# A ranking split in two: 14 of 16 rounds on the first 240 channels, and another order in an image's last tile

## What is computed

```python
x: (4, 256, 256, 256) float32                        # images, channels, rows, columns
v = _gn(x)                                           # group norm over 32 groups of 8 channels
s = 0.5 * (|dv/dx| + |dv/dy|) + 0.5 * |v|            # differences with [-1, 0, 1], zero padding
sp = s averaged over patches of 32 x 32              # 64 patches, a score for each channel
mask = 1 where a channel is among the 128 best of 256 in its patch, else 0
out = x + v * mask
```

## Time and profile before

| | |
|---|---|
| median of 3 timed runs | 2008.84 us (2007.42 to 2009.37) |
| the profiled execution's own time: its span | 2002.3 us |
| busy: PE, DVE, ACT, POOL | 69%, 77%, 81%, 78% of the span |
| DMA | 780.77 MB, mean 390 GB/s |
| the rankings: first `max` of each image | 382.2, 847.2, 1312.5 and 1773.0 us |

### The profile page before, as it was taken

The page is one execution under the profiler, slowest core; times in us unless marked ns, Lnnn a source line. Parts: engine busy times, 40 slices in busy tenths (PEclk is TensorE's granted clock), DMA queues, the critical chain, the costliest instruction groups (busy, mean ns, idle before and its releaser), DMA issues.

```text
span 2002.3 us, 16132 instructions
## 1 busy us (share of the span) xinstructions
PE 1380.7 (69%) x3528; PEld 675.7 (34%) x3528; DVE 1542.1 (77%) x2087; ACT 1629.1 (81%) x2437; POOL 1555.6 (78%) x1113
## 2 busy tenths in 40 slices
PE   5989989868768867857787687768688876820000
PEld 2444444434333433423333333334333333410000
DVE  7878898789898869879898977888888977872110
ACT  4999999898879888888898879889789887851643
POOL 7899899768787777758877868758878786746776
PEclk9999999988889878879888788889788887965555
DMA  5899899999999999998999999999999999969997
GB/s 252 330 399 369 333 360 392 354 403 424 429 432 430 422 362 433 390 415 365 428 430 429 432 399 389 433 389 386 430 430 432 426 400 390 381 267 397 397 368 270
DMA packets 72082, 780.77 MB, mean 390 GB/s; under 512 B 21883, under 2 KB 21883, under 8 KB 35648
## 3 DMA queue, kind: packets, MB, share of 16 engines
q1 hardware_dynamic: 40896, 723.54, 87.3%
q0 software_dynamic: 31104, 56.45, 7.5%
HBM read 568.33 MB, written 329.25 MB: 448 GB/s over the span
## 4 chain that ended last, share of the span: by engine, by line
issue 20%; DMA 19%; DVE 17%; POOL 16%; ACT 15%; PE 9%; DVEq 3%; POOLq 1%; ACTq 0%; SPq 0%
DVE stats L911 8%; DMA again<-in_x_dram 8%; POOL pair L349 5%; DMA ring<-in_x_dram 4%; ACT again L803 4%; DMA out_dram<-again 4%; DVE sums L938 4%; PE vertical L707 4%; ACT thrown L872 4%; PE vertical L709 4%; POOL pair L355 3%; DVEq L902 3%; ACT vertical L866 3%; DMA ring<-in_x_dram,pair 2%; POOL scratch L349 2%
## 5 line engine op out<-in xcount | busy, mean ns | idle before, releaser
L707 PE MATMUL vertical<-ring,plus 128*128 128x512 f32 (+1 forms) x1200 | 664.4, 638 | 241.9 <-ACT vertical L866 240.9
L349 POOL TENSOR_TENSOR pair<-ring 128x960 f32<-128x960 f32 x360 | 638.3, 1793 | 26.0 <-DVE scratch L1082 17.9
L709 PE MATMUL vertical<-ring,minus 128*128 128x512 f32 (+1 forms) x1200 | 634.0, 612 | 0.0
L911 DVE BATCH_NORM_STATS2 stats<-ring 128x6 f32<-128x512 f32 x960 | 582.4, 680 | 40.4 <-DMA ring<-in_x_dram 31.9
L872 ACT ACTIVATE thrown<-ring,record 128x1024 bf16<-128x1024 f32 x480 | 548.2, 1142 | 8.8
L938 DVE TENSOR_REDUCE sums<-pair 128x2 f32<-128x1920 f32 (+1 forms) x212 | 455.0, 2146 | 126.8 <-POOL pair L349 126.2
L803 ACT ACTIVATE again<-again,coef 128x1024 f32<-128x1024 f32 x324 | 374.4, 1227 | 107.2 <-DMA again<-in_x_dram 106.9
L707 PEld LDWEIGHTS vertical<-ring,plus 128*128 128x128 f32 x1200 | 240.9, 211 | 514.6 <-ACT vertical L866 292.4
L355 POOL TENSOR_TENSOR pair<-ring 128x960 f32<-128x960 f32 x120 | 270.5, 2254 | 141.8 <-DVE sums L938 116.3
L709 PEld LDWEIGHTS vertical<-ring,minus 128*128 128x128 f32 x1200 | 250.0, 208 | 295.5 <-issue 295.5
L349 POOL TENSOR_TENSOR scratch<-ring 128x960 f32<-128x960 f32 x120 | 215.3, 1794 | 152.8 <-ACT kept L822 103.3
(11 more groups left out here) (118 smaller groups left out, 1443.2 us busy)
## 6 DMA issues: line engine op xcount, KB each, us to landing
ring<-in_x_dram SPq DMA_DIRECT2D x59, 4096.0 KB, 20.4
again<-in_x_dram SPq DMA_DIRECT2D x89, 2048.0 KB, 16.6
out_dram<-again SPq DMA_DIRECT2D x89, 2048.0 KB, 16.3
out_dram<-in_x_dram SPq DMA_DIRECT2D x29, 2048.0 KB, 28.6
kept<-in_x_dram SPq DMA_DIRECT2D x4, 4096.0 KB, 22.7
out_dram<-kept SPq DMA_DIRECT2D x8, 2048.0 KB, 13.8
ring<-in_x_dram SPq DMA_DIRECT2D x4, 1024.0 KB, 7.8
out_dram<-ring SPq DMA_DIRECT2D x2, 2048.0 KB, 9.7
```

What stands on the lines that cost most here:

```text
L349: return nc.gpsimd.tensor_tensor(part.rearrange("p (r c) -> p r c", r=PATCH), xs[:, w, :, 2:], xs[:, w, :, 0:PATCH - 2], ALU.subtract)
L707: nc.tensor.matmul(v[:, first:end], plus[:], xs[:, first + 2 * PATCH:end + 2 * PATCH], start=True, stop=False)
L709: done = nc.tensor.matmul(v[:, first:end], minus[:], xs[:, first:end], start=False, stop=True)
L911: nc.vector.bn_stats(stats[:, k, :], buffer[:, k * BN:(k + 1) * BN])
```

## The change

Two things are moved. On GpSimd the first fill of PAIR_B in an image's last tile goes from ahead of the scales to behind the columns at the edge, so that the scales and the single patch come sooner; VectorE's sum of it goes behind `score_most`. And 14 of the 16 rounds run on the 240 columns already copied, ahead of the sums of PAIR_A 1 and PAIR_B 1; two rounds over all 256 columns follow in `rank`. The 112 that the 14 rounds take are among the best 128 of 256, as only 16 channels are still to come.

```diff
 ROUNDS = KEPT // 8
+ROUNDS_AHEAD = (KEPT - TILE_CH) // 8
...
                 fill(tile, kept, SINGLE, 0)
-                fill(tile, kept, PAIR_B, 0)
                 scales(image)
                 fill(tile, kept, SINGLE, 1)
                 columns_at_edge(tile, kept, RING)
+                fill(tile, kept, PAIR_B, 0)
                 fill(tile, kept, PAIR_A, 1)
                 fill(tile, kept, PAIR_B, 1)
...
                 next_statistics(2)
-                if not first_image:
-                    place_sum(tile, RING, PAIR_B, 0)
                 keep_sums(tile - 1, RING - 1, LAST - 1)
...
                 score_most(image)
-                place_sum(tile, RING, PAIR_A, 1)
+                if not first_image:
+                    place_sum(tile, RING, PAIR_B, 0)
                 dve.wait_ge(gathered, 2 * image + 1)
                 nc.vector.tensor_copy(left[:, 0:LAST * TILE_CH], score_bank[0:PATCHES, 0:LAST * TILE_CH])
+                settle()
+                choose(left[:, 0:LAST * TILE_CH], ROUNDS_AHEAD)
+                place_sum(tile, RING, PAIR_A, 1)
                 place_sum(tile, RING, PAIR_B, 1)
                 settle()
...
+            def choose(seen, rounds):
+
+                for _ in range(rounds):
+                    nc.vector.max(largest[:], seen)
+                    settle()
+                    nc.vector.match_replace(out=seen, in_to_replace=largest[:], in_values=seen, imm_value=-1.0)
+                    settle()
...
-                for _ in range(ROUNDS):
-                    nc.vector.max(largest[:], left)
-                    settle()
-                    nc.vector.match_replace(out=left, in_to_replace=largest[:], in_values=left, imm_value=-1.0)
-                    settle()
+                choose(left, ROUNDS - ROUNDS_AHEAD)
```

## The result

The changed kernel takes 2051.72 us (median of 5 runs, 2049.94 to 2052.91); the kernel before, on the same chip, 2009.37 (5 runs, 2007.42 to 2012.63). The ratio is 1.021, with a 95% interval of 1.0199 to 1.0221: slower by 42 us. The forecast was 2039.0, between 2022 and 2055. Direction and range hold; the number is that of the rival "nothing is caught up", 2051.1, and not the forecast's.

A forecast was written before the change was run, and what follows sets the result against it. No engine bounds the whole; what counts is which wait ends last near an image's end. Images 0 to 3 gave 11 + 9.9 + 12.8 - 3.2 = +30.5 us on the 2008.84 median: 2039.0, range 2022 to 2055.

The forecast's parts named there:

- nothing is caught up: Rival: ScalarE's full moves in images 0 to 2 reach the end, less image 3's gain; +42.3 us, 2051.1; chance 0.15.
- T: Start of the last tile's own score on VectorE; forecast to move +18.5, +12.9 and +14.1 us in images 0 to 2.
- What hangs on T: GpSimd's next-tile operations, TensorE's queue and ScalarE's first tile move whole with T, by 12.9 to 18.5 us.
- 11.2 us of cover, against 18.5: Image 0: transfers queued beyond the first kept store's issue hide 11.2 us of ScalarE's 18.5 us move; at least 7.3 lost.
- the term 11 of image 0: Image 0's loss: 7.3 us beyond the queue's cover and some 4 more when the queue runs dry again; taken as 11.
- T to kept tile: ScalarE's way from T to the kept tile in images 0 to 2, T + 25.9 in image 1, held to move whole.
- Image 1, +9.9: Image 1's loss: ScalarE comes 12.9 us later but gives up its 2.98 us wait for TensorE, so 9.9 is lost.
- Image 2, +12.8: Image 2's loss: T moves 14.1 us, with about 1.3 us of DMA queue as cover; 12.8 taken.
- Image 3, -3.2: Last image, no next tile: single patch and scores come sooner, the rounds end at 1786.6 instead of 1789.8; a 3.2 us gain.
- TensorE's clock: TensorE waits 14 us longer for the last score but cannot start colder than 1.2 GHz; nothing counted.
- The DMA queue hides most: Rival: DMA slack in an image's first tiles leaves only starvation beyond the queue to count; +15.5 us, 2024.3; chance 0.10.
- The ranking was the chain: Rival: the chain through the coefficients decides and next-tile work has slack; -6.2 us, 2002.6, faster; chance 0.03.

The follow-up runs named there:

- E7: The changed kernel with TensorE's mask moved ahead of the next tile's differences 2 and 3; 2051.29 us, ratio 1.0194 to the kernel before.
- E1: The changed kernel with the old order of fills and sums, so only the 14 rounds stand ahead; 2061.31 us, ratio 1.0255 to the kernel before.
- E6: The changed kernel with GpSimd's first fill of the next tile held until VectorE's choice is done; 2061.92 us, a single run.
- E4: The kernel before with seven further MAX8 behind the last copy, so behind T, in images 0 to 2; 2019.54 us, ratio 1.0038.
- E10: The changed kernel with image 0's last tile and ranking as before; 2028.34 us, ratio 1.0106 to the kernel before.
- E3: The kernel before with the whole change in image 3 only, images 0 to 2 as before; 2009.29 us, ratio 0.9992.

## Why the prediction was right or wrong

- **T.** +18.5, +12.9 and +14.1 were forecast, +18.1, +12.3 and +14.1 came. 14 rounds took 14.28 us for 14.3, partly by luck: image 0's 16 rounds took 16.75 us before (382.16 to 398.91), 1.05 each and not the 1.07 read in image 1, and a round on 240 columns saved 0.03 us and not 0.05. In image 0 the estimate of the gather had its cause right: VectorE waits 6.2 us there for it.
- **What hangs on T.** Forecast: GpSimd waits about 20 us, ScalarE about 17 (22 in image 0). Measured: 21.0, 16.4 and 16.4; 21.8, 18.3 and 18.4. VectorE's wait for the mask was to be some 10 and is 8.6 to 8.7, since the choice had become slower. `coef` at T + 18: 18.1 to 18.2.
- **The step that failed: "11.2 us of cover, against 18.5", and with it the term 11 of image 0.** Measured: 17.8. The mechanism was right, a queue that runs dry, and then runs dry once more. The cover was mis-sized. From the variance the kept tile moved by 20.0 us and the DMA engines stood 14.4, so the queue covered 5.6 and not 11.2. The sum on this trace: 5.6 of cover too much, 1.95 of fills' delay, less 0.4 on T and 0.8 on the second time without transfers (3.2 for 4), +6.3: from 7.3 + 4 to the 17.6 us in which DMA stands. The 5.6 is not a constant, though. The same working gives 9.3 in E7 (moved 20.0, stood 10.7), 8.9 in E1 (18.4 and 9.5) and 8.7 in E6 (23.0 and 14.3), and the interval grew by 17.5, 16.1 and 20.3 us all the same. Against the unchanged image 0 of the other traces (460.4 to 462.8) some 2 to 5 us of each of these moves were given back. So of a move of 20 us some 15 to 18 reach the end, where 18.5 was forecast to cost 11.

  Why the cover is less than 11.2 is shown in part. I had read it as the time from the first kept store's issue, 411.33, to the landing of the load that VectorE receives at 422.52. But most of the engines' work can be over before the last queued load has landed. In E7 VectorE receives that load at 430.14, ahead of any kept store:

```profile
430.14 7.22 DVE L912 BATCH_NORM_STATS2 stats<-ring 128x6 f32<-128x512 f32 x12 [1.44 <-DMA ring<-in_x_dram]
```
```profile
437.04 4.87 SPq L561 DMA_DIRECT2D out_dram<-kept  x2
```
```profile
420.00:424.00 4.00, 4.00 (x11) 1.90 (x11) 4.00 (x8) 3.27 (x5) 4.00 (x3) 1.00 1.04 440
424.00:428.00 4.00, 0.70 (x2) 0.00 (x0) 3.93 (x7) 3.97 (x8) 1.94 (x2) 1.00 0.63 270
428.00:432.00 4.00, 3.87 (x11) 2.04 (x12) 2.09 (x6) 4.00 (x9) 0.00 (x0) 1.00 0.02 8
```

  The shares of 0.63 and 0.02 put the end of the engines' work near 426.6, 3.5 us ahead of the landing. One would think that before the change the kept stores also held up the load beside which they moved (they took 16.3 us from issue to landing there, and 8.4 in the changed kernel, alone). The load's landing doesn't show it: 65.8 us behind the variance before, 64.1 to 68.1 in the seven other kernels whose kept stores come ahead of it, and 67.7 in E7, where no store is beside it. Why the changed kernel's queue ended 3 to 4 us sooner after the variance than E7's stays open.
- **A size off: two microseconds of mutual delay.** The forecast held T to kept tile "unchanged". It grew by 1.95 us in each of three images, 5.8 together, because two rounds behind T bring the choice down onto GpSimd's fills. The order of instructions showed that both would start within 6 us of T; the forecast used the durations of the trace of before, in which they ran apart (E6).
- **Image 1, +9.9.** Near, and the reason given fits: ScalarE's 2.98 us of waiting are gone. T and fills moved the kept tile by 14.3 and the interval grew by 10.9, so 3.4 were given up. VectorE's statistics moved by 7.0 only, less than `coef`, as its gap at the loop's return shrank from 6.29 to 3.33. No run isolates it. **Image 2, +12.8:** 14.1 and 1.95 make 16.05, and 16.2 came. No cover of 1.3 us by the queue can be seen.
- **Image 3, -3.2.** Came as -3.35. The parts hold too: counted from the variance, the single patch is summed at 7.8 us instead of 12.6 (the forecast's 1754 is 7.9), and the scores are copied at 17.4 instead of 22.8 (17.8). Of the rounds only two stand behind T.
- **TensorE's clock.** Nothing was counted, and rightly. After 20.01 us of waiting the two matmuls at 880.11 take 2.08 us, and the granted clock is 0.50 from 880 to 885; after the 3.51 us of before they took 2.08 as well.
- **The rivals.** *Nothing is caught up* had the time, 2051.1, for half of the reason: in its sum image 1 gives nothing back, image 0's small cover is missing, and it knows nothing of the fills' delay; the errors, 3.4 and some 2 against 5.8, nearly cancel. *The DMA queue hides most* fell: the queue ran dry in image 0 after 5.6 us, and in images 1 and 2 the moves arrived whole but for some 3 us in image 1. *The ranking was the chain* fell: in E7 TensorE takes the mask at once, `coef` comes 8 us sooner, and the time stays. But E4 shows it to be nearer than I wrote: `coef` had a margin of some 2 us in image 2, not the 3.6 at the kept tile, because it is the statistics behind it that are wanted, not the coefficients.

The corrected sum on the trace is 17.8 + 10.9 + 16.2 - 3.35, about +41.5, for 42 in the runs.

**Open.** Whether VectorE's 3 to 6 us without a releaser at the loop's return cost anything of themselves was not tried. No experiment moves the kept stores alone, with T in its place; that they carry the loss rests on E7, E10 and the times in which DMA stands.

## What to carry to other kernels

Before you put work into a waiting time of one engine, look up what the next instruction of that engine releases on the others: here 14.3 us of ranking were cheap on VectorE and held GpSimd, TensorE, ScalarE and the stores. Where the DMA engines are full, count the time in which they will stand, and don't take the landing of the last queued load for the end of the cover: here it overstated it by 2 to 6 us. When two chains end within a few microseconds of each other, shortening or lengthening one tells you nothing of the other; move one with the other in its place (E4, E7) before you price a move between them, and compare with a second trace of unchanged code (here E3) before you read a wait of 2 us as an effect.

## What the runs showed of the hardware that was not expected

**VectorE and GpSimd hold each other up.** In the changed kernel the eight halves of the choice took between 1.21 and 3.24 us for the same operation and shape, and in E6 between 1.21 and 1.22. The view of that one line, changed kernel and then E6 (shortest, median and longest in ns, then first and last start):

```profile
L1117 DVE SCALAR_TENSOR_TENSOR scratch<-scratch,same_channel x8: 1209/2221/3242, 405.9 to 1836.0; 64x1024 bf16<-64x1024 f32 x8
```
```profile
L1118 DVE SCALAR_TENSOR_TENSOR scratch<-scratch,same_channel x8: 1209/1214/1218, 405.9 to 1844.8; 64x1024 bf16<-64x1024 f32 x8
```

The operation has two inputs in SBUF. GpSimd's fills beside it took 0.97 us longer each (3.20 for 2.23, 2.76 for 1.78). The writing of `coef` took 1.61 us at 897.69 where it takes 0.23, with one input only: it ended at 899.30, and the three fills that GpSimd had begun at 893.95 ended at 899.22. The Trainium skill (SBUF — State Buffer, the section on SBUF's two separate sides) says that a VectorE operation with two SBUF inputs, or in a mode with two ports, and a GpSimd operation take the pair of ports that they share one after the other, each for its whole length. The rows agree in size for the choice: its worst half is 2.0 us longer, about one fill. Whether the writing of `coef` runs in such a mode no run here tells.

**A gap that nothing releases.** At the return of the loop VectorE stood 6.29 us before image 2's first sums in the kernel before (876.18), 3.33 in the changed kernel (904.53), and 6.47 and then 3.15 in E4. Only image 1 shows it; in images 0 and 2 the same place has 0.24 or 0.25. Over the twelve traces it is 3.1 to 3.4 us in the four kernels in which VectorE had waited 8.7 us or more for the mask just before (changed, E1, E6, E10), and 6.1 to 6.6 in the other eight, where that wait was at most 1.0. No run shows why.
